# Encoder stages of a sixteen-layer kernel: the late piece of a step moves ahead of two groups of transposes on TensorE

## The reference

```python
gate_logits = x.mean(axis=1) @ gate_w.T + gate_b
_, top_idx = jax.lax.top_k(gate_logits, K)
...
def _encoder_layer(x, iw, ib, ow, ob, l1w, l1b, l2w, l2b, n1w, n1b, n2w, n2b):
    qkv = x @ iw.T + ib
    ...
    scores = jnp.einsum('bhqd,bhkd->bhqk', q, k) / scale
    attn = jax.nn.softmax(scores, axis=-1)
    o = jnp.einsum('bhqk,bhkd->bhqd', attn, v).transpose(0, 2, 1, 3).reshape(b, s, d)
    o = o @ ow.T + ob
    x = _layernorm(x + o, n1w, n1b)
    ff = jax.nn.relu(x @ l1w.T + l1b) @ l2w.T + l2b
    return _layernorm(x + ff, n2w, n2b)
```

## The kernel before

| step c | early piece on PE | late piece on PE | what DVE does behind the norm of the attention output |
|---|---|---|---|
| 0 | `t1`: turn x1 (L1329) | `qk`: project q and k (L475, L476) | moments of the second norm (L1479, L1482) |
| 1 | `t`: turn the attention output (L601) | `f1`: first half of the hidden layer (L1333) | second norm (L1522) |
| 2 | `y`: output projection (L609) | `f2`: second half of it (L1333) | moments of the first norm (L1479, L1482), gated sum into x (L1528) |
| 3 | `v`: project v (L479) | `f3`: second feed-forward matmul (L1338) | first norm (L1508), which POOL scales and shifts (L1290, L1292) for `t1`; adding `f3` (L1537) |

## Time and profile before

### The profile page before, as it was taken

One profiled execution on the slowest core, in us unless ns is written; L12 is line 12 of the kernel. 1 busy time (PEld: TensorE's weight loads), 2 busy tenths in 40 slices (PEclk: granted clock), 3 DMA queues, 4 the chain that ended last, 5 costly groups with the idle time before them and its releaser, 6 DMA issues. The chain is left out here.

```text
span 2944.2 us, 62888 instructions
## 1 busy us (share of the span) xinstructions
PE 2626.4 (89%) x24286; PEld 1750.9 (59%) x24286; DVE 1947.8 (66%) x4549; ACT 1401.5 (48%) x2887; POOL 1086.1 (37%) x1384
## 2 busy tenths in 40 slices
PE   7999789989699879897887899997999989889998
PEld 2344457756467656465555577774666657556665
DVE  7888746757566677634774577765777747557775
ACT  5555234456244335322663355544555545445653
POOL 4787545324345313313112434430222346312223
PEclk9899789999799989889999999998999999999999
DMA  2000200011000001100111000002222211112221
GB/s 85 1 1 0 82 22 23 10 26 31 26 19 23 5 3 50 70 29 19 31 24 32 17 1 1 1 1 69 62 91 71 69 32 31 61 46 77 78 88 49
DMA packets 62020, 107.28 MB, mean 36 GB/s; under 512 B 7978, under 2 KB 46582, under 8 KB 60960
## 3 DMA queue, kind: packets, MB, share of 16 engines
q1 hardware_dynamic: 56352, 94.80, 10.6%
q0 software_dynamic: 5376, 8.47, 1.0%
HBM read 80.17 MB, written 23.86 MB: 35 GB/s over the span
## 5 line engine op out<-in xcount | busy, mean ns | idle before, releaser
L617 ACT ACTIVATE s_sT<-s_R 128x1024 f32<-128x1024 f32 (+2 forms) x448 | 402.6, 945 | 180.4 <-PE s_R L548 180.2
L659 DVE TENSOR_REDUCE s_negm<-s_R 128x4 f32<-128x1024 f32 (+1 forms) x320 | 359.5, 1166 | 88.9 <-PE s_R L517 87.0
L517 PE MATMUL s_R<-s_qk 32*128 32x256 f32 (+2 forms) x3584 | 243.1, 384 | 46.2 <-ACT s_sT L617 25.3
L548 PE MATMUL s_R<-s_qA,s_qk 32*128 32x256 f32 (+2 forms) x3584 | 240.9, 382 | 12.4 <-DVE s_negm L659 7.2
L568 PE MATMUL s_OB<-s_sT,s_v 128*32 128x256 f32 (+2 forms) x3584 | 224.5, 368 | 7.5 <-ACT s_sT L617 3.8
L691 DVE TENSOR_TENSOR s_qA<-s_qk,s_OB 128x256 f32<-128x256 f32 x224 | 94.4, 421 | 201.3 <-PE s_OB L591 193.7
L517 PEld LDWEIGHTS s_R<-s_qk 32*128 32x128 f32 x3584 | 155.3, 186 | 103.5 <-issue 67.1
L548 PEld LDWEIGHTS s_R<-s_qA,s_qk 32*128 32x128 f32 x3584 | 164.5, 185 | 65.1 <-issue 55.8
L624 ACT ACTIVATE s_oc<-s_OB 128x256 f32<-128x256 f32 x224 | 85.8, 383 | 230.1 <-PE s_OB L568 229.8
L1599 POOL TENSOR_TENSOR s_pr<-s_pr,s_rinv 128x1024 f32<-128x1024 f32 x64 | 121.1, 1892 | 186.5 <-DVE s_rinv L1710 186.5
L2940 POOL TENSOR_TENSOR all_hT<-s0s_hs,s0s_cb 128x1024 f32<-128x1024 f32 x64 | 150.7, 2354 | 29.7 <-PE s0s_Y L2887 14.3
(11 more groups left out here) (614 smaller groups left out, 6267.6 us busy)
## 6 DMA issues: line engine op xcount, KB each, us to landing
s_wB<-enc_b SPq DMA_DIRECT2D x32, 962.5 KB, 4.7
s_scratch<-s_pk SPq DMA_DIRECT2D x58, 256.0 KB, 2.0
s_qk<-s_scratch SPq DMA_DIRECT2D x232, 64.0 KB
s_wA<-enc_a SPq DMA_DIRECT2D x32, 194.0 KB, 4.1
big<-moe SPq DMA_DIRECT2D x2, 2347.0 KB, 10.7
big<-routed SPq DMA_DIRECT2D x2, 2312.0 KB
all_W<-weights SPq DMA_DIRECT2D x1, 2201.0 KB, 16.4
all_W<-weights SPq DMA_DIRECT2D x1, 2200.5 KB, 11.7
```

The source lines that it names most:

```text
L517: last = pe.matmul(S[h][:, a.keys_at(t)], b.qk[rows, r % 2, 0, c, t * P:(t + 1) * P], b.qk[rows, r % 2, 1, c, lo:hi], start=(t == 0), stop ...
L548: last = pe.matmul(b.R[:, a.turned_at(u, h // 2), :][:, h % 2, a.at(kt)], b.qk[rows, r % 2, 1, c, kt * P:(kt + 1) * P], b.qA[rows, u % 2, ...
L617: act.activation(b.sT[:, u % (a.lag + 1), 2 * p:2 * p + 2, 0:a.width], b.R[:, a.turned_at(u, p), 0:a.width], ACT.Exp).then_inc(s.expd, 1)
L659: return dve.tensor_reduce(b.negm[:, u % 2, :, at].rearrange("p t h -> p h t"), S[:, :, 0:a.key_width].rearrange("p h (t k) -> p h t k", t ...
```

## The change

In the loop of `encoder_stage` on PE, the late piece of a step is issued ahead of the two turnings instead of behind them. No instruction is added or removed, and no wait is changed; DVE, ACT, POOL and SP keep their instructions and their order.

```diff
@@ -1374,12 +1374,12 @@
                         keep_busy(pe, g, b.R[:, 0, :], 7)
                     if u >= U:
                         keep_busy(pe, g, b.R[:, a.pair(4 * U, 2), :][:, 0, :], 3)
+                    for item in a.late(u):
+                        other(item)
                     if u + 1 < U:
                         slot_turn_max_pe(pe, g, a, b, u + 1)
                     if 0 <= u - a.lag < U:
                         slot_turn_out_pe(pe, g, a, b, u - a.lag)
-                    for item in a.late(u):
-                        other(item)
```

## The result

| | before, us | changed, us |
|---|---|---|
| median of the timed runs | 2942.31 | 3008.29 |
| lowest and highest | 2936.19, 2942.46 | 3007.12, 3008.79 |
| span of the profiled execution | 2944.2 | 3006.1 |

The changed kernel takes 1.0232 times as long (95% interval 1.0218 to 1.0246): 66 us more, against a forecast of 83.

What follows compares the result with a forecast made beforehand. PE was taken as the bound, busy 21.51 of 21.59 us a unit. Steps +2.61 and neighbours 0.20 gave +2.81 a unit, 75.9 us over 27; with first-stage extra, +83: 3025 us, range 3000 to 3050.

Steps and rivals of the forecast that it cites:

- the four waits: PE would wait for DVE at the turned scores in steps 0, 1 and 3, and at `f2`; chance 0.80.
- 0 to 1: L591 of step 0 to that of step 1: DVE's moments and `f1` in the loop, 5.46 us.
- 1 to 2: L591 of step 1 to that of step 2: `f2` waits until DVE has read `y`, 5.83 us.
- 2 to 3: L591 of step 2 to that of step 3: moments, gated sum and `f3` in the loop, 6.83 us.
- 3 to 0: L591 of step 3 to that of step 0: norm, addition of `f3` and `qk` in the loop, 6.08 us.
- the matmuls beside new neighbours: Late pieces behind turned scores cost PE more, first turnings may give some back: +0.05 us a step, 0.20 a unit.
- It is late with it, not later, so I add nothing: Step 0: `t1` waits for POOL until 3.23 us after L591, turned scores start at 3.77; nothing added.
- The extra of the first stage: First encoder stage: the next layer's norm lengthens DVE's list seven times, 8.5 us, less about 1 it costs already.
- this rival: Slower clock in the encoder stages: at 0.85, at most 102 us more, up to 3127 us; chance 0.07.
- Part of the loss is taken up: Encoder waits shorter than the row intervals, half the loss stays: 1.4 us a unit, +38 us, 2980; chance 0.09.
- no loss: Turned scores need not wait for the maxima, loop 19.7 us, PE stays full: 2942 us; chance 0.02.
- Faster: The moved piece fills PE's idle holes in the encoder stages: 8 us gained, 2934 us; chance 0.02.

Runs made afterwards that it cites:

- the last experiment: Changed kernel, with DVE's moments and gated sum behind the next maxima, `y` read between the maxima halves, first norm ahead of adding the maxima: 2971.11 us.
- The kernel with the extra operation: Changed kernel plus one more DVE addition (128x256) in each encoder step, ahead of the maxima: 3048.47 us, ratio 1.0374.
- the experiment with the output first: Changed kernel with PV's output turned ahead of the late piece, and DVE's output norm and norm work ahead of adding the maxima: 2945.45 us.

## Why the prediction was right, and where the sum was off

*The mechanism.* Each of the four waits came at the place and with the releaser that the prediction named, except that in step 0 it is `t1` that waits for POOL. The turned scores start 3.15 us after L591 in step 1 (forecast 3.15), 3.55 in step 3 (3.60) and 3.71 in step 0 (3.77); `f2` starts at 4.50 (4.59). L582 has no idle time, DVE has none ahead of the maxima, and its idle time ahead of L691 grew. The unit lies above the 23.5 us under which the theory would have been wrong, and below the 24.2 to 24.6 forecast. PE's busy share in the stages is 90 and 92%, not 88: the unit is shorter than forecast, and for the same matmuls the records give 21.91 us busy where they gave 21.51.

*The sum.* It was made as 24.40 us a unit; 23.81 came. By steps, forecast with the 0.05 for neighbours, then measured from L591 to L591:

| interval | forecast | measured | what was smaller |
|---|---|---|---|
| 0 to 1 | 5.51 | 5.41 | neighbours 0.10 |
| 1 to 2 | 5.88 | 5.69 | neighbours 0.10, norm 0.08 |
| 2 to 3 | 6.88 | 6.73 | neighbours 0.10, gated sum 0.09; maxima to turned scores 0.03 longer |
| 3 to 0 | 6.13 | 5.98 | neighbours 0.10, norm 0.08, `f3`'s addition 0.08; POOL 0.09 longer |

The step that failed in size is "the matmuls beside new neighbours": "I take +0.05 a step". In the waiting ring they give back about 0.05 a step instead. From the turned scores to L591 around `f1` it is 2.27 us (2.31 forecast without neighbours), around `f3` 3.18 (3.23): the first turning takes 0.21 to 0.22 behind a late piece where it took 0.28 behind the turned scores, the "give-back" that the prediction had named as an estimate. The expected +0.10 for a projection behind scores did not come: in step 0 the projections take 0.97 us (2740.08 to the turning at 2741.05), as behind the turnings, and not the 1.06 of the earlier trace rows. What became dearer is L517 right behind L591, 0.32 us (2735.29 to 2735.61) in place of 0.22 for the late piece there; it lies under the wait for DVE and so costs nothing here. Taken together, 0.10 more at L517 and 0.05 less up to L591 are the forecast's +0.05 a step, and the 0.2 us a unit of the last experiment: the size was right for PE's work, but the sum put it into a ring that holds only the part that became cheaper.

The second term is DVE's list. "Each norm 0.59" and "gated sum 0.45" were durations of rows; from start to start it is 0.51 (2736.50 to 2737.01) and 0.36 (2730.38 to 2730.74), since the next instruction starts before the row of the last one ends. In the earlier trace rows the next instruction had been waiting for PE, so no such distance was to be read there; but DVE's addition (L691) showed the overlap in the trace of before, with a row of 0.42 us and the next instruction 0.33 us after its start (2669.49 to 2669.82).

"It is late with it, not later, so I add nothing" was the third, and small. POOL's shift ends 3.23 us after L591 (2737.89 + 0.63, less 2735.29), as forecast, but from there to the turned scores it is 0.48 us (PE's start 0.15, the transposes 0.33) and not 0.22. DVE alone would have let them start at 2.28 + 1.34 = 3.62; POOL makes it 3.71.

*From the unit to the time.* By stages the forecast was 13.5 x 2.81 = 37.9 us for the second and 7.5 more, 45.4, for the first; 31.6 and 38.0 came. The extra of the first stage is thus 6.4 for 7.5, by two errors that cancel: the next layer's norm adds more (365.50 - 355.96 = 9.5 us between the stages, for 8.5), and it had cost 3.2 already (327.52 - 324.36, for 1). The count of 13.5 units hid part of the error too: 0.59 us less a unit would be 8.0 us, but the second stage is only 6.3 under its forecast, since the steps that fill and drain it and the units with a slower POOL add some 1.7. The encoder stages give 13.7 us of what the profiled execution (3007.80) lies under the forecast of 3029; 7.1 are those ahead of the first stage, 4.8 of them the stretch with the higher clock, which the forecast could not know.

*The clock.* Both encoder stretches have 1.00, the upper of the two levels, with idle gaps of 0.2 to 1.1 us in every step. The Trainium skill ("TensorE: Matmul & The Clock Gate", section "A second HAM failure mode: psum-queue depth-cycling") tells of a kernel in which frequent short idle times let the clock swing. The trace of the changed kernel shows no such swing, so the row of 131 us in the earlier trace rows was the better guide to it. The kernel with the extra operation shows two falls in its first stage, behind waits of 0.9 and 1.0 us in one step, so this rival was nearer than that row let it seem.

*The other rivals.* "Part of the loss is taken up" (2980) and "no loss" needed a list or a wait that is shorter than its row; the lists were shorter by at most 0.16 us a step, not by half of the loss. "Faster" needed holes to fill; the only ones in the new trace are those that the change made.

## What to carry to other kernels

Before moving a piece on the bound engine, find the instruction that starts the other engine's list and the one that waits for its end. Work between the two is free cover, and the same work outside them adds to the ring: here one DVE addition a step cost 9 us inside the cover and 40 us without it. Add such a ring up from distances between starts, not from durations, and look for the loss one step behind the moved piece.

## What the hardware did unexpectedly

- The cost of two small transposes hangs on their place, not on which they are: behind the turned scores 0.28 us, behind a full-height late piece 0.22, ahead of the 32-row scores 0.31. In the experiment with the output first, L591 has the 0.27 to 0.28 and L582 the 0.31. The weight loads (PEld) go with it: behind the turned scores L582's load starts with its first matmul (2668.72 before), behind a late piece 0.22 us ahead of it (2722.44 for 2722.66 in the changed kernel).
- POOL's operations on 128x256 take 0.64 us in some units and 0.73 in others, with the same operands. Where POOL decides, `t1` then waits 1.10 instead of 0.91 us, and the unit takes 23.99 instead of 23.80. No run shows why.
